# Feed-forward x turned on VectorE in 32x32 blocks by way of DRAM, in place of TensorE transposes

## The chip, the cores and the metric

One core of one Trainium2 chip. The metric is the device time of one execution in microseconds (us). Three executions of the kernel before took 1996.22, 1997.45 and 1999.36 us; the median is 1997.45.

## What is computed

One transformer block on x of 8192 tokens x 512 channels, all float32:

```python
mod = silu(c) @ wmod                       # sa, ca, ga, sb, cb, gb, 512 each
h = layernorm(x) * (1 + ca) + sa
x = x + ga * linear_attention(h)           # causal, 16 heads of 32
h = layernorm(x) * (1 + cb) + sb
gate = h @ w_gate.T / 127                  # hidden size 1536
up = h @ w_up.T / 127
x = x + gb * ((silu(gate) * up) @ w_down.T / 127)
```

The change is about the second layernorm: its result h is wanted with channels on the partitions, while x is loaded with tokens on the partitions.

## The kernel before

The attention works through 16 groups of 512 tokens, the feed-forward behind it through 8 groups G of 1024 tokens (8 tiles of 128). The attention's output goes to the DRAM tensor `x_mid`; the feed-forward reads it from there. Every engine has its program written out by hand, in order, with semaphores between them; groups 1 to 6 of the feed-forward are a loop.

A feed-forward group has 12 **steps** q, one for each block of 128 hidden values, and two **down** phases, one after step 5 and one after step 11. For a step TensorE makes seven products of four matmuls of 512 columns in the order p1(q), p7(q-1), p2(q), p5(q), p4(q-1), p6(q), p3(q) (a Strassen-Winograd scheme: operands are B11, B21, B22 and four sums T1 to T4 of channel and token halves, each for k = 0 and 1). A down phase has 8 down products (one a token tile) of 12 matmuls of 512 columns, in four banks `dn`; p7 and p4 of the last step lie between the first ones, and p1, p2 and p5 of the next half or group lie before the eighth. Bank i % 4 is free for down product i when product i - 4 has been multiplied by the gate row gb (`gate_y`, VectorE).

For a step ScalarE copies partial sums out of PSUM (`save_p1`, `save_p5`, `save_u2`), makes the two silus (`silu1`, `silu2`) and rounds the products to their high parts (`h_high`). VectorE makes `add_c22(q-1)`, `add_c11(q)`, `times_gate2(q-1)`, `times_gate1(q-1)`, then whatever is put aside for this step, and `add_c12(q)`. GpSimd makes the low parts of h (`h_low`) and the residual sums (`residual`), SP issues all DMAs. In the trace add_c11 is L1704, add_c12 L1710, add_c22 L1715, times_gate1 L1721, times_gate2 L1729 and gate_y L1736 on VectorE; silu2 is L1590 and save_u2 L1578 on ScalarE. TensorE's p products are L1868 and its down products L1925.

Operands of the next group are made while this one runs:

- SP loads x of group G + 2 in the second down phase of G (`load_x`, L1405) into eight tiles: four in `xg`, two in `z_exp`, two in `z_relu`.
- VectorE makes statistics in steps 2 to 5 (`norm_stats`, L1681), `norm_var` in step 5, GpSimd the power -1/2 (`rstd_of`, L1492), and VectorE normalises in place, two tiles at a time, behind add_c12(6) and in steps 7, 8 and 9 (`norm_x`, L1697).
- TensorE turns: a **turn** is four transposes of 128x128 into one bank, 512 tokens of 128 channels. There are eight a group (`turn`, L1936): one behind each of the steps 8 to 11, three behind p4(11) and one behind the third down product.
- ScalarE evacuates each turn with scale and bias of the modulation (`evacuate`, L1562): the first three in steps 9, 10 and 11 between h_high and silu2, the fourth behind silu2(11), the others later. Then it rounds the operands to high parts (`high`, L1547).
- VectorE makes the sums T1 to T4 (`sum_of`, L1671) and the low parts (`low`, L1675) behind step 11, mixed with gate_y of the second down phase and, at the end, add_c11 of the next group. T1 for k = 0 waits for three evacuations, the other sums for four.

Group 0 of the feed-forward gets its x in the last two groups of the attention: SP loads each half in one DMA (L404) when its tiles have been stored, VectorE makes its statistics (L757) between other work of the attention, and TensorE turns it (L1097, L1105). Behind this load on SP's queue stand the load of a residual tile (L311), the four stores of a block of k (L319), weights and the load of k (L328).

## Time and profile before

| | |
|---|---|
| runs | 1996.22, 1997.45, 1999.36 us |
| profiled execution | 1998.45 us |
| its span | 1996.7 us |
| granted TensorE clock | 0.998 (mean) |
| TensorE / VectorE / ScalarE / GpSimd busy | 98 / 72 / 45 / 44% |
| DMA | 309.81 MB, mean 155 GB/s |

The span runs from the first to the last instruction of the profiled execution; its time is 1.75 us longer, and 1.0 us above the median of the three. The first feed-forward products lie near 990 us, so about half of the span is attention and half feed-forward. Busy shares are averages over stages with different limits, and a TensorE that is busy need not be at its peak.

### The profile page before, as it was taken

The numbers are of one execution on the slowest core, as the hardware profiler recorded it, in microseconds if no ns is written. First come the engines' busy times: TensorE is split into PE (matmuls) and PEld (weight loads), VectorE is DVE, ScalarE is ACT, GpSimd is POOL, SyncE is SP. The second block draws the span as 40 slices with busy tenths as digits, with TensorE's granted clock in tenths as the row PEclk, the third lists the DMA queues.
The fourth block names the chain that finished last, engine by engine and source line by source line (L and its number), as shares of the span: only waits on it lengthen the run. The fifth ranks groups of instructions, "written<-read, shape, count | busy, mean of one in ns | idle before, by whom it ended". The sixth has DMA issues, their size and how long they took to land. (4 is left out here: it accounts for less than half of the span.)

```text
span 1996.7 us, 43856 instructions
## 1 busy us (share of the span) xinstructions
PE 1960.6 (98%) x16008; PEld 1591.9 (80%) x16008; DVE 1443.1 (72%) x2386; ACT 905.7 (45%) x1542; POOL 877.4 (44%) x718
## 2 busy tenths in 40 slices
PE   7999999999999999999899999999999999999999
PEld 4788888888888888887678888788888888888887
DVE  7977888878788878787865857658576585765744
ACT  5443444344444434443344535445354453544533
POOL 2533544444544444453334443444434444344444
PEclk9999999999999999999999999999999999999999
DMA  7223333444434434432575654656546565465553
GB/s 268 69 91 102 115 123 119 135 130 133 135 100 133 128 125 135 127 110 90 179 263 176 207 187 145 214 170 209 186 144 215 171 210 186 144 214 174 169 168 106
DMA packets 202521, 309.81 MB, mean 155 GB/s; under 512 B 16145, under 2 KB 72977, under 8 KB 202386
## 3 DMA queue, kind: packets, MB, share of 16 engines
q1 hardware_dynamic: 201858, 306.78, 48.1%
q8 instruction: 107, 1.75, 0.4%
q10 hardware_dynamic: 528, 1.05, 0.1%
q14 instruction: 28, 0.23, 0.0%
HBM read 225.19 MB, written 82.58 MB: 154 GB/s over the span
## 5 line engine op out<-in xcount | busy, mean ns | idle before, releaser
L1497 POOL TENSOR_TENSOR h_lo<-y_rows,h_hi 128x512 fp32r<-128x512 f32 x192 | 246.5, 1301 | 367.6 <-ACT h_hi L1595 367.6
L461 POOL TENSOR_TENSOR x_res<-y,x_res 128x512 f32<-128x512 f32 x64 | 86.6, 1353 | 294.0 <-DVE y L872 283.5
L851 DVE TENSOR_TENSOR probs<-sc,causal 128x512 f32<-128x512 f32 x256 | 158.5, 681 | 3.8 <-PE sc L1156 2.6
L612 ACT ACTIVATE z_exp<-pj,qk_neg 128x512 f32<-128x512 f32 x128 | 87.7, 686 | 161.5 <-PE pj L1137 158.0
L1137 PE MATMUL pj<-xt_hi,w_hi 128*128 128x512 f32 x512 | 145.9, 406 | 5.7 <-DVE a_t L861 4.7
L1925 PE MATMUL sc<-wd,h_hi 128*128 128x512 f32 x384 | 150.7, 392 | 0.0
L1925 PE MATMUL sc<-wd,h_lo 128*128 128x512 f32 x384 | 149.6, 389 | 0.0
L450 POOL TENSOR_TENSOR a_lo<-a_t,a_hi 128x512 fp32r<-128x512 f32 x60 | 82.2, 1370 | 144.8 <-ACT a_hi L626 144.8
L1137 PE MATMUL pj<-xt_lo,w_hi 128*128 128x512 f32 x512 | 138.1, 391 | 1.8 <-DVE xt_lo L789 1.8
L1137 PE MATMUL pj<-xt_hi,w_lo 128*128 128x512 f32 x512 | 138.1, 392 | 0.0
L1710 DVE TENSOR_TENSOR r_den<-pj,k_tok 128x512 f32<-128x512 f32 x96 | 66.3, 691 | 97.9 <-ACT k_tok L1578 52.2
L1595 ACT ACTIVATE h_hi<-y_rows 128x512 fp32r<-128x512 f32 x192 | 119.0, 620 | 24.9 <-DVE y_rows L1729 13.4
L1573 ACT ACTIVATE k_tok<-sc 128x512 f32<-128x512 f32 x96 | 56.2, 585 | 158.7 <-PE sc L1868 158.7
L445 POOL TENSOR_TENSOR prod<-k_sum,qt 128x512 f32<-128x512 f32 x64 | 94.1, 1471 | 61.4 <-DVE qt L797 42.5
L597 ACT ACTIVATE xf<-sc,mod_col 128x512 f32<-128x512 f32 x64 | 49.8, 778 | 152.7 <-PE sc L1097 152.7
L1137 PEld LDWEIGHTS pj<-xt_hi,w_hi 128*128 128x128 f32 x512 | 91.8, 189 | 33.1 <-DVE a_t L861 11.0
L1137 PEld LDWEIGHTS pj<-xt_lo,w_hi 128*128 128x128 f32 x512 | 96.2, 188 | 23.3 <-DVE xt_lo L789 2.2
L1568 ACT ACTIVATE kv_diag<-pj 128x512 f32<-128x512 f32 x96 | 57.4, 598 | 123.9 <-PE pj L1868 122.9
L1137 PEld LDWEIGHTS pj<-xt_hi,w_lo 128*128 128x128 f32 x512 | 96.7, 189 | 20.9
L1583 ACT ACTIVATE k_sum<-r_den 128x512 f32<-128x512 f32 x96 | 60.7, 632 | 107.7 <-DVE y_rows L1721 95.0
L1721 DVE TENSOR_TENSOR y_rows<-sc,k_sum 128x512 f32<-128x512 f32 x96 | 66.3, 691 | 55.6 <-PE sc L1868 55.6
L1715 DVE TENSOR_TENSOR bv_row<-sc,kv_diag 128x512 f32<-128x512 f32 x96 | 66.3, 691 | 54.8 <-PE sc L1868 54.8
(248 smaller groups left out, 5390.4 us busy)
## 6 DMA issues: line engine op xcount, KB each, us to landing
w_hi<-parts SPq DMA_DIRECT2D x48, 1024.0 KB, 5.4
w_lo<-parts SPq DMA_DIRECT2D x48, 1024.0 KB, 5.4
x_mid<-x_res SPq DMA_DIRECT2D x96, 256.0 KB, 2.8
x_res<-in_L_attn_x SPq DMA_DIRECT2D x64, 256.0 KB, 2.8
k_dram<-k_block SPq DMA_DIRECT2D x252, 64.0 KB
xg<-in_L_attn_x SPq DMA_DIRECT2D x15, 1024.0 KB, 7.4
x_res<-x_mid SPq DMA_DIRECT2D x60, 256.0 KB, 3.9
full<-x_mid SPq DMA_DIRECT2D x60, 256.0 KB, 3.7
```

The costliest lines, as they stand in the source:

```text
L445: pool.tensor_tensor(out=prod[:, c % 2, :], in0=k_sum[:, c % 2, :], in1=qt[parity][:, c, :], op=ALU.mult).then_inc(prod_ready, 1)
L450: pool.tensor_tensor(out=a_lo[:, :], in0=a_t[:, :], in1=a_hi[:, :].bitcast(F32), op=ALU.subtract).then_inc(a_lo_ready, 1)
L461: pool.tensor_tensor(out=x_res[:, slot, :], in0=y[:, :], in1=x_res[:, slot, :], op=ALU.add).then_inc(y_ready, 1)
L612: act.activation(z_exp[:, n % 2, :], pj[:, n % 2, :], ACT.Relu, bias=qk_neg[:, 1 - kind, c:c + 1], scale=-scale).then_inc(below_ready, 1)
L851: dve.tensor_tensor(out=probs[:, h, :].rearrange("p (c i) -> p c i", c=C), in0=sc[:, h, :].rearrange("p (c i) -> p c i", c=C), in1=causal[ ...
L1137: mm = pe.matmul(to, w[:, k, at:at + P], xt[:, k, :], start=(i == 0), stop=(i == len(passes) - 1))
L1497: pool.tensor_tensor(out=h_lo[b], in0=h[i], in1=h_hi[b].bitcast(F32), op=ALU.subtract).then_inc(h_lo_ready, 1)
L1595: act.activation(h_hi[q % 6 * 2 + i], h[i], ACT.Copy).then_inc(h_hi_ready, 1)
L1710: dve.tensor_tensor(out=c12, in0=sums[1], in1=s12, op=ALU.add).then_inc(c12_ready, 1)
L1715: dve.tensor_tensor(out=c22, in0=xs[q % 2], in1=s5, op=ALU.add).then_inc(c22_ready, 1)
L1721: dve.tensor_tensor(out=h[0], in0=xs[q % 2], in1=gate[0], op=ALU.mult).then_inc(h1_ready, 1)
L1925: mm = pe.matmul(dn[i % 4], as_(part[j * 2 + t // GT][:, rows]), as_(wd[half * 6 + j]), start=(j == 0 and part is h_hi), stop=(j == 5 and ...
```

## The change

x of the next group is no longer transposed by TensorE. SP stores each normalised half (512 tokens) to a new DRAM tensor `xn_dram` and loads it back in 16 blocks a partition, so that one VectorE transpose of 32x32 blocks, 128x2048 in place, puts channels on the partitions. The channels come out regrouped (32 of each quarter on each partition quarter), so the host permutes the rows of the gate and up weights and of the modulation alike, and group 0, which TensorE still turns, is loaded in regrouped order, in pieces of 32 channels (128 bytes). ScalarE's evacuations read SBUF instead of PSUM. `z_exp` and `z_relu` become two halves of one tensor `z`, so that a half of x is one tensor.

```diff
@@ sync, attention: x of feed-forward group 0 @@
-                sp.dma_start(xg[:, :, :], mid_groups[half, :, :, :]).then_inc(x_in, 16)
+                for t in range(GT):
+                    for c in range(C):
+                        sp.dma_start(xg[:, t, c * P:(c + 1) * P].rearrange("p (h e) -> p h e", h=HPC),
+                                     mid_groups[half, :, t, :].rearrange("p (h c e) -> c p h e", h=HPC, c=C)[c]
+                                     ).then_inc(x_in, 16)
@@ sync, feed-forward @@
+        def save_xn(G, second):
+            wait(sp, xn_ready, G * 4 + (2 * second - 2))
+            sp.dma_start(xn_dram[second * GN:(second + 1) * GN, :].rearrange("(t p) d -> p t d", p=P),
+                         xg_halves[second][:, :, :]).then_inc(xn_out[second], 16)
+        def load_blocks(G, second):
+            wait(sp, xn_out[second], G * 16)
+            for h in range(HPC):
+                sp.dma_start(xg_halves[second][h * E:(h + 1) * E, :, :].rearrange("p t (b x) -> p (t b) x", x=P),
+                             xn_dram[second * GN:(second + 1) * GN, h * P:(h + 1) * P].rearrange("(b i) x -> i b x", i=E)
+                             ).then_inc(xb_in[second], 16)
...
                     if not last or q + 4 < HB:
                         load_parts(G, q + 4)
+                    if not last and q in (5, 6):
+                        save_xn(G + 1, q - 5)
+                    if not last and q in (7, 8):
+                        load_blocks(G + 1, q - 7)
@@ scalar @@
-                step(G, q, (lambda i=q - 9: evacuate(G + 1, i, dn[i])) if ahead and q >= 9 else nothing)
+                step(G, q, (lambda: (evacuate(G + 1, 0), evacuate(G + 1, 1))) if ahead and q == 11 else nothing)
...
-            evacuate(G + 1, 3, dn[3])
+            evacuate(G + 1, 2)
+            evacuate(G + 1, 3)
@@ vector @@
+        def turn(G, second):
+            wait(dve, xb_in[second], G * (16 * HPC))
+            blocks = xg_halves[second][:, :, :].rearrange("p t d -> p (t d)")
+            dve.transpose(blocks, blocks).then_inc(xt_ps, 1)
...
-                if ahead and not first and 2 <= q < 6:
-                    norm_stats(G + 1, q - 2)
-                if ahead and q == 5:
+                if ahead and not first and 1 <= q < 5:
+                    norm_stats(G + 1, q - 1)
+                if ahead and q == (5 if first else 4):
                     norm_var(G + 1)
-                if ahead and 7 <= q < 10:
-                    norm_x(G + 1, q - 6)
+                if ahead and q >= 10:
+                    turn(G + 1, q - 10)
...
             times_gate1(G, 5)
+            if ahead:
+                norm_x(G + 1, 0)
+                norm_x(G + 1, 1)
             for i in range(FT - 1):
                 gate_y(G, i)
+                if ahead and i in (3, 4):
+                    norm_x(G + 1, i - 1)
             add_c11(G, 6)
             gate_y(G, FT - 1)
             add_c12(G, 6)
-            if ahead:
-                norm_x(G + 1, 0)
@@ tensor: turn() and its eight calls with their waits are gone @@
```

GpSimd's `rstd_of` moves from behind step 5's low parts to ahead of step 4's (step 5's in group 0).

VectorE at the end of the steps of a looped group, from times_gate2(9) to T1 of the next group. Before:

```order
L1729 TENSOR_TENSOR y_rows<-bv_row,gabo_row 128x512
L1721 TENSOR_TENSOR y_rows<-sc,k_sum 128x512
L1710 TENSOR_TENSOR r_den<-pj,k_tok 128x512
L1715 TENSOR_TENSOR bv_row<-sc,kv_diag 128x512
L1704 TENSOR_TENSOR r_den<-pj,k_tok 128x512
L1729 TENSOR_TENSOR y_rows<-bv_row,gabo_row 128x512
L1721 TENSOR_TENSOR y_rows<-sc,k_sum 128x512
L1710 TENSOR_TENSOR r_den<-pj,k_tok 128x512
L1671 TENSOR_TENSOR full<-xf 128x512
```

Now, from times_gate2(9) on (L1730 is the transpose, L1742 add_c12, L1747 add_c22, L1736 add_c11, L1761 and L1753 the products with the gate, L1697 T1):

```order
L1761 TENSOR_TENSOR y_rows<-bv_row,gabo_row 128x512
L1753 TENSOR_TENSOR y_rows<-sc,k_sum 128x512
L1730 STREAM_TRANSPOSE xg<-xg 128x2048
L1742 TENSOR_TENSOR r_den<-pj,k_tok 128x512
L1747 TENSOR_TENSOR bv_row<-sc,kv_diag 128x512
L1736 TENSOR_TENSOR r_den<-pj,k_tok 128x512
L1761 TENSOR_TENSOR y_rows<-bv_row,gabo_row 128x512
L1753 TENSOR_TENSOR y_rows<-sc,k_sum 128x512
L1730 STREAM_TRANSPOSE z<-z 128x2048
L1742 TENSOR_TENSOR r_den<-pj,k_tok 128x512
L1697 TENSOR_TENSOR full<-xf 128x512
```

A transpose of 2048 columns stands ahead of add_c12 in step 10 and in step 11; what follows step 11 has its old order.

ScalarE in step 11 and behind it, from silu1(11) (L1583) to the fourth evacuation (L1562; L1590 is silu2). Before:

```order
L1583 ACTIVATE k_sum<-r_den 128x512
L1595 ACTIVATE h_hi<-y_rows 128x512
L1578 ACTIVATE k_tok<-sc 128x512
L1595 ACTIVATE h_hi<-y_rows 128x512
L1562 ACTIVATE xf<-sc,mod_col 128x512
L1590 ACTIVATE gabo_row<-r_den 128x512
L1562 ACTIVATE r_den<-state,mod_col 128x512
```

Now, from silu1(11) (L1608) to the fourth evacuation (L1587; L1615 is silu2):

```order
L1608 ACTIVATE k_sum<-r_den 128x512
L1620 ACTIVATE h_hi<-y_rows 128x512
L1603 ACTIVATE k_tok<-sc 128x512
L1620 ACTIVATE h_hi<-y_rows 128x512
L1587 ACTIVATE xf<-xg,mod_col 128x512
L1587 ACTIVATE r_den<-xg,mod_col 128x512
L1615 ACTIVATE gabo_row<-r_den 128x512
L1587 ACTIVATE xf<-z,mod_col 128x512
L1587 ACTIVATE r_den<-z,mod_col 128x512
```

One evacuation stood ahead of silu2(11) and one behind it, two others in earlier steps; now two stand ahead of it and two behind.

SP in the attention's last groups, around the load of x for group 0. Before, and now:

```order
L328 DMA k_tok<-k_dram 128x512
L62 REGISTER_ALU
L62 COMPARE_AND_BRANCH
L404 DMA xg<-x_mid 128x4x512
L311 DMA x_res<-in_L_attn_x 128x512
L319 DMA k_dram<-k_block 32x4x128 x4
L332 DMA x_mid<-x_res 128x512
L328 DMA r_den<-k_dram 128x512
```

```order
L329 DMA k_tok<-k_dram 128x512
L62 REGISTER_ALU
L62 COMPARE_AND_BRANCH
L407 DMA xg<-x_mid 128x4x32 x16
L312 DMA x_res<-in_L_attn_x 128x512
L320 DMA k_dram<-k_block 32x4x128 x4
L333 DMA x_mid<-x_res 128x512
L329 DMA r_den<-k_dram 128x512
```

One DMA has become sixteen; the order behind it is the same.

## Rows read from the trace of the kernel before

**Rows 1.** The page, part 1: busy time, share of the span and instructions.
```profile
PE 1960.6 (98%) x16008; PEld 1591.9 (80%) x16008; DVE 1443.1 (72%) x2386; ACT 905.7 (45%) x1542; POOL 877.4 (44%) x718
```

**Rows 2.** Timeline of TensorE, 1200 to 1206: start us, us, engine, line, operation, out<-in, count.
```profile
1201.09 0.62 PE L1868 MATMUL pj<-xt_hi,w_hi 128*128 128x512 f32 x2
1201.55 0.60 PE L1936 MATMUL num<-ident,xg 128*128 128x128 f32 x4
...
1202.45 0.63 PE L1868 MATMUL sc<-xt_hi,w_lo 128*128 128x512 f32 x2
```

**Rows 3.** Timelines of TensorE and of ScalarE, 1265 to 1269.
```profile
1266.52 0.61 PE L1868 MATMUL sc<-xt_hi,w_hi 128*128 128x512 f32 x2
...
1267.58 0.63 PE L1868 MATMUL sc<-xt_lo,w_lo 128*128 128x512 f32 x2
...
1266.38 0.58 ACT L1578 ACTIVATE k_tok<-sc 128x512 f32<-128x512 f32 x1
```

**Rows 4.** Timeline of TensorE, 1225 to 1275.
```profile
1227.09 0.67 PE L1868 MATMUL sc<-w_hi 128*128 128x512 f32 x2
...
1242.61 0.46 PE L1925 MATMUL sc<-wd,h_hi 128*128 128x512 f32 x1
...
1250.86 0.73 PE L1868 MATMUL sc<-w_lo,w_hi 128*128 128x512 f32 x2
```

**Rows 5.** Timeline of VectorE, 1220 to 1275.
```profile
1220.54 0.69 DVE L1721 TENSOR_TENSOR y_rows<-sc,k_sum 128x512 f32<-128x512 f32 x1 [0.61 <-PE sc L1868]
...
1224.18 1.47 DVE L1671 TENSOR_TENSOR full<-xf 128x512 f32<-128x512 f32 x1 [0.44 <-ACT xf L1562]
...
1226.30 0.68 DVE L1715 TENSOR_TENSOR bv_row<-sc,kv_diag 128x512 f32<-128x512 f32 x1
...
1229.30 1.47 DVE L1671 TENSOR_TENSOR full<-r_den,full 128x512 f32<-128x512 f32 x1
1230.70 1.77 DVE L1675 TENSOR_TENSOR xt_hi<-full,w_lo 128x512 fp32r<-128x512 f32 x1
...
1241.84 0.68 DVE L1736 TENSOR_TENSOR a_t<-sc,ga_row 128x512 f32<-128x512 f32 x1
...
1250.04 0.68 DVE L1704 TENSOR_TENSOR r_den<-pj,k_tok 128x512 f32<-128x512 f32 x1
```

**Rows 6.** The instructions of line 1936: duration ns min/median/max, first and last start us.
```profile
L1936 PE MATMUL num<-ident,xg x28: 270/272/273, 1076.5 to 1825.7; 128*128 128x128 f32 x28
```

**Rows 7.** The tile k_block, same columns.
```profile
L845 DVE STREAM_TRANSPOSE k_block<-kt x63: 662/670/714, 63.4 to 972.8; 128x512 f32<-128x512 f32 x63
```

**Rows 8.** Timeline of ScalarE, 1220 to 1275.
```profile
1223.38 0.77 ACT L1562 ACTIVATE xf<-sc,mod_col 128x512 f32<-128x512 f32 x1
1224.04 0.63 ACT L1590 ACTIVATE gabo_row<-r_den 128x512 f32<-128x512 f32 x1
1224.56 0.77 ACT L1562 ACTIVATE r_den<-state,mod_col 128x512 f32<-128x512 f32 x1
```

**Rows 9.** DMA issues: line, queue, count, size of one, us to landing.
```profile
parts<-r_den SPq DMA_DIRECT2D x48, 256.0 KB, 2.4
```

**Rows 10.** Timeline of SP's DMA issues, 880 to 980.
```profile
895.78 0.39 SPq L404 DMA_DIRECT2D xg<-x_mid  x1
...
946.67 1.77 SPq L319 DMA_DIRECT2D k_dram<-k_block  x4
...
956.47 0.39 SPq L404 DMA_DIRECT2D xg<-x_mid  x1
...
973.58 3.04 SPq L319 DMA_DIRECT2D k_dram<-k_block  x4
```

**Rows 11.** Timeline of VectorE, 880 to 1012.
```profile
908.02 1.86 DVE L757 BATCH_NORM_STATS2 stats<-xg 128x6 f32<-128x512 f32 x3
...
962.17 1.29 DVE L757 BATCH_NORM_STATS2 stats<-xg 128x6 f32<-128x512 f32 x2 [0.45 <-DMA xg<-x_mid]
...
965.28 0.42 DVE L861 TENSOR_TENSOR a_t<-num,r_den 128x256 f32<-128x256 f32 x1 [0.96 <-PE pj L1181]
```

More of the change, by code:

```diff
@@ L1321, in attention, with feed_forward @@
     return Programs(sync, gpsimd, scalar, vector, tensor), signals, shared
-def feed_forward(sem, later, ident, mod_col, half_neg, norm, gb_dram, parts, att, shared, x_mid, out):
+def feed_forward(sem, later, mod_col, half_neg, norm, gb_dram, parts, att, shared, x_mid, xn_dram, out):
     stats, mean_var, var_eps, rstd = norm[1:5]
-    xg, xf, h_hi, h_lo, (blocks, filled), b_hi, b_lo, full, wd, total, saved, gate, h, y, x_res, gb_row, xs, sums, dn = shared
+    xg, xg_halves, xf, h_hi, h_lo, (blocks, filled), b_hi, b_lo, full, wd, total, saved, gate, h, y, x_res, gb_row, xs, sums, dn = shared
     c11, c12, c22 = total
@@ L1636, in body @@
             high(G + 1, T4, 0)
-            for i, bank in ((4, sums[0]), (5, sums[1]), (6, xs[0]), (7, xs[1])):
-                evacuate(G + 1, i, bank)
+            for i in range(4, 8):
+                evacuate(G + 1, i)
             for op in (B11, B21, T1, T2, B22, T3, T4):
@@ L1928, in down @@
                 mm.then_inc(dn_ps, 1)
-        def turn(G, i, bank):
-            k, which = divmod(i, 4)
-            c, second = (k, k + 2, k, k + 2)[which], which // 2
-            wait(pe, xn_ready, G * 4 + (2 * second - 2))
-            for t in range(GT):
-                mm = pe.transpose(bank[:, t * P:(t + 1) * P], xg[second * GT + t][:, c * P:(c + 1) * P], ident[:, :])
-            mm.then_inc(xt_ps, 1)
         def step(G, q):
```

57 lines of the change are left out of this document (23 added, 34 removed).

## The prediction

> **What bounds the kernel now.** I read the page first: TensorE is busy 98% of the span, VectorE 72% [rows 1]. The edit takes 224 transposes off TensorE, so at first sight their time is the gain. The timeline of TensorE gives it. Two matmuls take 0.455 us from start to start. Where four transposes (one turn) lie between p3 of a step and p1 of the next, 1201.09 to 1202.45 is 1.36 us instead of 0.91: a turn costs 0.45 us [rows 2]. But a boundary without a turn is not free either: 1266.52 to 1267.58 is 1.06 us, 0.15 too many, since p7 waits for ScalarE's save_u2, which ends at 1266.96 [rows 3]. So a turn at a step boundary is worth 0.30 us. Of the 8 turns of a group, 3 are followed by a further step and 5 by a down product: 3 x 0.30 + 5 x 0.45 = 3.15 us, in 7 groups 22.0 us. That is the ceiling.
>
> Then I asked what ends TensorE's waits where the last five turns are. Three places touch. p4 of step 11 starts at 1227.09; the c22 that it needs is a VectorE sum that starts at 1226.30 and takes 0.68. The down product of bank 2 starts at 1242.61; the gating that frees its bank starts at 1241.84 and takes 0.68, so it ends 0.09 earlier. p6 of the next group starts at 1250.86; its c11 starts at 1250.04 and ends 0.14 earlier [rows 4, 5]. Between 1224.18 and 1250.7 VectorE has no gap: eight sums, fourteen low parts, six gatings, c22, two products with the gate and c11 run back to back, most of them 0.6 us apart. So in the tail of a group VectorE and TensorE are level, and **VectorE's row of work sets when the next group starts**. Removing TensorE work there gives nothing unless this row also starts or ends earlier. The group's period is 124.9 us: (1825.7 - 1076.5) / 6 [rows 6].
>
> **The change, part by part.**
> *Boundaries of steps 8 to 10.* The turns leave three boundaries, where TensorE is the bound: -0.30 x 3 = -0.9 us per group.
> *The turn on VectorE.* 128x512 costs 0.67 us (63 times, 662 to 714 ns) [rows 7]. Of that some 0.13 is overhead (the next instruction starts 0.6 after it), so 128x2048 is about 4 x 0.535 + 0.13 = 2.3 us. Bounds: 4 x 0.54 = 2.1 below; above, 4 x 1.77 = 7.1, if it were held like the sum with two SBUF inputs at 1230.70, which ran beside a GpSimd instruction [rows 5]. I take 2.3, as it has one input and its own row never shows more than 714 ns. In step 10 it stands after times_gate1 and before add_c12. From the end of p4, which releases times_gate1, TensorE has p6, p3, p1, p7, p2 = 20 matmuls x 0.228 = 4.55 us before p5 wants that sum; 0.69 + 2.3 + 0.69 = 3.7 fit, with 0.9 to spare. Cost 0, up to a turn of about 3.1 us. The Trainium skill speaks against this part: "VectorE: DVE Perf Modes", rules for kernel authors, sends a 128x128 transpose to TensorE where a PSUM destination will do, and its table of transpose paths has 311 ns for 128 bf16 columns on VectorE; by that, as an estimate, a turn would be 16 x 0.311 = 5.0 us. The row of this trace says less than half of it.
> *The evacuations.* This is where the saving goes. Now the third evacuation (1223.38, 0.77 us) comes before silu2 (1224.04), and the first sum, T1, starts at 1224.18, just behind it; the fourth starts at 1224.56 [rows 5, 8]. After the change the first and second stand where the third was and the third and fourth come behind silu2: one evacuation (0.66 from start to start), silu2 (0.52) and again one evacuation (0.66) more before T1, so T1 starts 1.84 us later, at 1226.0. silu2's own sum is ready in time: times_gate1 at 1220.54, turn at 1221.15, add_c12 from 1223.4 to 1224.1. Reading SBUF instead of PSUM I take as equal; bounds 0.52 (the pitch to silu2's successor) and 0.77 each, which is -0.4 to +0.3 us on T1.
> *The row of VectorE behind it.* T1 takes 1.47 us now because GpSimd is in a low part; at 1226.0 GpSimd is done, and it takes 0.68: -0.8. The two long ones that follow (1229.30 and 1230.70) stay, as GpSimd's next low parts move along with their products. The order of the row is the same. So it ends 1.84 - 0.8 = about 1.0 us later, bounds 0.4 and 1.9.
> *Sum per group:* -0.9 + 1.0 = +0.1 us (-0.9 to +1.0), in 7 groups +0.5 us (-6 to +7). TensorE gets to p4, to bank 0 and to bank 2 early and waits there for c22 and the gatings.
> *Normalising and statistics moved.* Four products 0.5 us apart come before gating 0, which waits anyway for its down product more than 5 us; two pairs between gatings 3 and 5 fall in gaps; statistics one step earlier need x by the group's first step, and it is loaded during the down products before; norm_var in step 4 uses about as much as the turn in step 10. Each 0; if they are late, add_c12 is late next.
> *Store and loads through DRAM.* One 1 MB store and four 256 KB loads for each half are issued by SP behind loads of weights; the loads go out two steps, 13 us, before their turn, and 512-byte pieces are no problem: 256 KB in 512 of them lands in 2.4 us [rows 9]. A weight load is issued more than three steps before use. 0.
> *End of the attention.* SP's single load of x for a group of 512 tokens (956.47, landing just after 962) becomes 16 loads of 64 KB in 128-byte pieces [rows 10]. VectorE's statistics are already waiting for it: 0.45 us, start at 962.17 [rows 11]. Four loads of 64 KB take 1.77 us now (0.48 apart), and 3.04 us (0.90) at worst [rows 10]; I take 0.55, as nothing there has so many pieces. The last lands at 956.5 + 15 x 0.55 + 2.4 = 967.1, so VectorE stands 4.9 us longer, of which the gap of 0.96 us at 965.28 [rows 11] and some tenths are taken back: **+3.8 us**. The residual load, the k store and weights queue behind on SP, by 8 us, but their users have moved by nearly 4 and had as much in hand. Bounds: +2.7 at 0.48; at 0.90 the last lands at 972.4, +9.1, and the first such load (895.78, statistics at 908.02) lands at 911.7, +3.7 more: +12.8.
>
> Sum: +0.5 - 0.3 (group 0 runs outside the loop, its boundaries give a little more) + 3.8 = +4.0 us. Against the profiled execution's 1998.45 us that is 2002.5; against the median of the runs, which is 1.0 us below it, 2001.5 us.
>
> **Rivals.**
> *A, the work of TensorE is the bound after all* (faster). Then the full 22.0 us come: 1997.45 - 22.0 + 3.8 = 1979 us. For it: 98% against 72%. Against it: the three touching places. It decides where VectorE's row from T1 to c11 gets 3 us shorter or starts that much earlier.
> *B, VectorE's row starts no later* (evacuations from SBUF quick, or fewer collisions with GpSimd): the boundaries' 0.9 x 7 = 6.3 us come: 1995 us, no change.
> *C, the small pieces bind.* The queue takes 0.90 us a load or more: 1997.45 + 0.2 + 12.8 = 2010.5 us. No row shows 128-byte data. The Trainium skill, "DMA: Bandwidth & Descriptors", specifications, says that below 512 bytes a transfer is not at line rate and is done as a read-modify-write; its figure of 0.95 us for 64 KB would put the sixteenth, as an estimate, at 974.
> *D, the turn is late or slow.* With 7.1 us instead of 2.3 it would overrun step 10 by 4.0 and shift T1 by a further 4.2 us: 7 x 8 = 57 us, 2058; a turn of 4 us would give 7 x 1.9 = 13 us, 2015. Nothing in the rows of the transpose speaks for it; it starts at about 3.0 us.
> *E, the change doesn't do what it says:* excluded for TensorE, the order has no transposes left there.
>
> **How the numbers follow.** Forecast (+0.1 a group, tail +3 to +6) 0.52; A 0.10; B 0.18; C 0.13; D 0.07. A measurement here tells 0.2% (4 us) from no change, so the borders are 1993.45 and 2001.45, and the forecast lies on the upper one. Faster: A, and a third of B with quick evacuations and a short tail, 0.17. Slower: C, D and about half of the forecast's cases, 0.47. Same: 0.36. The range leaves out A and most of D: 1992 to 2011, with B's lower end and C in it.
>
> **What would show it.** Right: 14 transposes of 2.2 to 2.4 us; step periods of 6.54 us throughout; a group's period of 124.3 to 125.6; T1 1.8 us later behind times_gate1 of step 10; TensorE waiting over 1 us for c22 at p4 and for a gating at bank 0; statistics in the last attention group waiting about 5 us for x. Wrong: a period near 121.8 (A), or waits for xn_dram before a transpose, or a transpose over 3 us (D).

## The result and the profile after

The changed kernel takes 2013.28 us (median of four runs, 2011.39 to 2015.96) against 1997.39 us for the kernel before in the same series: a ratio of 1.0079, 95% interval 1.0062 to 1.0097. It is slower by about 16 us, and outside the predicted range. Its profiled execution took 2011.44 us, with a span of 2009.7 us and a mean granted clock of 0.993 [before: 1998.45, 1996.7, 0.998].

The page of the changed kernel, parts 1 and 3, answers to [rows 1]:

```profile
PE 1945.9 (97%) x15784; PEld 1572.1 (78%) x15784; DVE 1476.3 (73%) x2400; ACT 908.8 (45%) x1542; POOL 883.9 (44%) x718
...
q1 hardware_dynamic: 254658, 336.15, 55.3%
```

TensorE lost its 224 transposes, and VectorE has 14 more instructions. They are as long as forecast, though each of the 14 ran beside a GpSimd instruction (groups of VectorE's instructions; last come the mean ns of one and the idle time before them). What was not forecast stands at the end of the first line:

```profile
L1730 DVE STREAM_TRANSPOSE z<-z 128x2048 f32<-128x2048 f32 x7 | 16.2, 2310 | 6.2 <-DMA z<-xn_dram 6.2
L1730 DVE STREAM_TRANSPOSE xg<-xg 128x2048 f32<-128x2048 f32 x7 | 16.1, 2303 | 0.0
```

**Where the time came from.** The starts of add_c11 of each group's first step make a ruler for the feed-forward. They are read off VectorE's timeline (line 1704 before, line 1736 after):

```
                 group 0   then the seven periods to groups 1 ... 7
before            995.59   129.37 125.08 125.13 124.67 124.70 124.64 124.67
after            1004.82   129.63 124.63 127.72 124.53 124.80 124.60 125.06
```

So of the 13.0 us between the two profiled executions 9.2 arose before the feed-forward began and 3.8 in it: 2.6 in the single period 127.72, 1.0 from the last group's first step to the end. The other periods are as before or some tenths shorter. Two places, then.

*The end of the attention.* SP's timeline has the two series of 16 loads, [rows 10] before (start us, us, queue, line, out<-in, count):

```profile
895.74 11.73 SPq L407 DMA_DIRECT2D xg<-x_mid  x16
...
960.96 11.16 SPq L407 DMA_DIRECT2D xg<-x_mid  x16
```

That is 0.73 and 0.70 us per load, not 0.55. VectorE's statistics wait for them (its timeline, [rows 11] before, where the first had no such wait and the second 0.45 us):

```profile
909.33 1.88 DVE L762 BATCH_NORM_STATS2 stats<-xg 128x6 f32<-128x512 f32 x3 [1.28 <-DMA xg<-x_mid]
...
974.06 1.29 DVE L762 BATCH_NORM_STATS2 stats<-xg 128x6 f32<-128x512 f32 x2 [8.34 <-DMA xg<-x_mid]
```

Both series count. At 890 us, ahead of the first, VectorE is where it was in the kernel before, within 0.1 us; at 925 us, behind the first, it is 4.0 us late, and behind the second 9.2. Of the 4.0 only 1.3 is the wait above. The rest comes in two longer waits of VectorE behind it, for TensorE (2.25 us instead of 1.33) and for ScalarE (2.86 instead of 1.08); meanwhile the residual load that stands behind the series on SP's queue goes out at 907.5 instead of 897.2. What holds up the two engines was not followed further.

*The long period.* Group 2's last step on VectorE, answering to [rows 5]:

```profile
1353.92 0.69 DVE L1753 TENSOR_TENSOR y_rows<-sc,k_sum 128x512 f32<-128x512 f32 x1 [0.39 <-PE sc L1903]
1357.98 2.31 DVE L1730 STREAM_TRANSPOSE z<-z 128x2048 f32<-128x2048 f32 x1 [3.37 <-DMA z<-xn_dram]
1360.22 0.65 DVE L1742 TENSOR_TENSOR r_den<-pj,k_tok 128x512 f32<-128x512 f32 x1
1362.27 0.69 DVE L1697 TENSOR_TENSOR full<-xf 128x512 f32<-128x512 f32 x1 [1.40 <-ACT xf L1587]
1363.07 0.69 DVE L1697 TENSOR_TENSOR full<-r_den,full 128x512 f32<-128x512 f32 x1
1363.68 0.68 DVE L1747 TENSOR_TENSOR bv_row<-sc,kv_diag 128x512 f32<-128x512 f32 x1
```

The turn of the second half waits 3.37 us for its blocks. Everything behind it moves: T1 (1362.27), then c22 (1363.68), and TensorE's p4 behind that (its timeline, [rows 4] before):

```profile
1364.41 0.73 PE L1903 MATMUL sc<-w_hi 128*128 128x512 f32 x2 [4.27 <-DVE bv_row L1747]
...
1365.71 0.63 PE L1960 MATMUL sc<-wd,h_hi 128*128 128x512 f32 x1
1366.14 0.63 PE L1960 MATMUL sc<-wd,h_lo 128*128 128x512 f32 x1
```

Behind the stall the matmuls start 0.43 us apart instead of 0.23. The granted clock says why. Windows of that stretch (PE, PEld, DVE, ACT and POOL busy, then granted clock, DMA share, GB/s):

```profile
1356.00:1360.00 4.00, 4.00 (x19) 3.10 (x17) 2.02 (x1) 2.28 (x4) 2.49 (x2) 1.00 1.03 373
1360.00:1364.00 4.00, 0.14 (x1) 0.00 (x0) 2.50 (x5) 2.88 (x5) 0.00 (x0) 1.00 0.16 65
1364.00:1368.00 4.00, 3.59 (x10) 2.82 (x11) 4.00 (x6) 3.74 (x7) 1.43 (x2) 0.64 0.14 19
1368.00:1372.00 4.00, 4.00 (x18) 3.31 (x17) 4.00 (x6) 3.83 (x6) 1.29 (x1) 0.93 0.65 243
```

So 4.27 us of idling were followed by a stretch at the lower of TensorE's two levels, 1.2 GHz. No 2 us window between 1000 and 1880 of the profiled kernel before is under 0.95 of full speed.

SP's timeline tells why the blocks are late. The four loads of the second half took 6.68 us to issue:

```profile
1340.75 0.93 SPq L1399 DMA_DIRECT2D w_hi<-parts  x1
1341.72 6.68 SPq L1423 DMA_DIRECT2D z<-xn_dram  x4
1348.51 3.28 SPq L1399 DMA_DIRECT2D w_lo<-parts  x1
```

The last of them went out near 1348 and the blocks were there at 1357.9. SP's DMA issues have 8.6 and 9.9 us as the median from a load's own issue to its landing:

```profile
xg<-xn_dram SPq DMA_DIRECT2D x28, 256.0 KB, 8.6
z<-xn_dram SPq DMA_DIRECT2D x28, 256.0 KB, 9.9
```

The theory to test: **16 small-piece loads delay the end of the attention; blocks that land late, by amounts that vary, cost the rest, with a stretch at half clock behind each long stall of TensorE; the feed-forward's own balance is as forecast.**

### The profile page after: what moved, and what is told of

Its sections match the earlier page's. It is cut to its first block and busy times, and to the rows that moved or that the text cites. A ratio compares the mean times of both kernels' runs of the same rounds, so it can differ in the third digit from the quotient of the medians.

```text
span 2009.7 us, 43425 instructions
## 1 busy us (share of the span) xinstructions
PE 1945.9 (97%) x15784; PEld 1572.1 (78%) x15784; DVE 1476.3 (73%) x2400; ACT 908.8 (45%) x1542; POOL 883.9 (44%) x718
## 5 line engine op out<-in xcount | busy, mean ns | idle before, releaser
L617 ACT ACTIVATE z<-pj,qk_neg 128x512 f32<-128x512 f32 x128 | 87.8, 686 | 164.0 <-PE pj L1142 153.9
L1742 DVE TENSOR_TENSOR r_den<-pj,k_tok 128x512 f32<-128x512 f32 x96 | 65.7, 685 | 92.4 <-ACT k_tok L1603 68.5
L1608 ACT ACTIVATE k_sum<-r_den 128x512 f32<-128x512 f32 x96 | 60.7, 632 | 106.3 <-DVE y_rows L1753 95.5
L1747 DVE TENSOR_TENSOR bv_row<-sc,kv_diag 128x512 f32<-128x512 f32 x96 | 66.2, 689 | 53.6 <-PE sc L1903 53.5
L1753 DVE TENSOR_TENSOR y_rows<-sc,k_sum 128x512 f32<-128x512 f32 x96 | 66.3, 690 | 49.8 <-PE sc L1903 49.5
```

The costliest lines, as they stand in the source:

```text
L617: act.activation(z_exp[:, n % 2, :], pj[:, n % 2, :], ACT.Relu, bias=qk_neg[:, 1 - kind, c:c + 1], scale=-scale).then_inc(below_ready, 1)
L1747: dve.tensor_tensor(out=c22, in0=xs[q % 2], in1=s5, op=ALU.add).then_inc(c22_ready, 1)
L1753: dve.tensor_tensor(out=h[0], in0=xs[q % 2], in1=gate[0], op=ALU.mult).then_inc(h1_ready, 1)
```

## The experiments

All edits start from the changed kernel unless said otherwise. Ratios are against the kernel before in the same series, with 95% intervals.

### One load per half instead of 16

```
-                for t in range(GT):
-                    for c in range(C):
-                        sp.dma_start(xg[:, t, c * P:(c + 1) * P]..., ...[c]).then_inc(x_in, 16)
+                sp.dma_start(xg[:, :, :], mid_groups[half, :, :, :]).then_inc(x_in, 16)
```

> The changed kernel, with group 0's x fetched by one DMA per half as before instead of 16 with 128-byte pieces; the channels of group 0 are then not regrouped, so its values are not the reference's. Theory (the 16 loads delay the end of attention by the 9.2 us that add_c11(0, 0) moved, 995.59 to 1004.82): add_c11(0, 0) near 995.6 and the time 9 us under the changed kernel's 2011.4, so about 2002, some 4 to 5 us above the kernel before. Rival (the loads only show the shift, which the feed-forward's code or DMAs make): add_c11(0, 0) stays past 1003 and the time is within 2 us of the changed kernel's.

add_c11(0, 0) started at 996.42, so the loads do make the delay. But the time did not follow: 2014.46 us (five runs, 2004.17 to 2017.19), ratio 1.0085 [1.0068, 1.0102]. Only the profiled execution, the fastest, is near the forecast 2002; the others have a granted clock down to 0.990. In it the late blocks sit in groups 0 and 1, not 2: periods 132.75 and 125.89, waits for xn_dram of up to 3.5 us, stretches at the lower clock from 1104 and from 1232. The forecast of the time failed because I had taken the late blocks of one profile as the cost in every run.

### Blocks one step earlier

```
+                    if not last and q in (6, 7):
+                        load_blocks(G + 1, q - 6)
                     if not last or q + 4 < HB:
                         load_parts(G, q + 4)
-                    if not last and q in (5, 6):
-                        save_xn(G + 1, q - 5)
-                    if not last and q in (7, 8):
-                        load_blocks(G + 1, q - 7)
+                    if not last and q == 5:
+                        save_xn(G + 1, 0)
...
                     store(G, i)
+                    if not last and i == 5:
+                        save_xn(G + 1, 1)
```

> The changed kernel, with the blocks of the next group saved and loaded one step earlier, the second half's save before the first's step 6 loads and each pair of block loads ahead of that step's load of parts on SP. Theory (group periods of 124.6 are the floor, the 127.7 of group 2 is a late block): no wait of the transpose for xn_dram of over 0.3 us in any group, no stretch at a granted clock of about 0.6 after steps 10 and 11, every group at 124.5 to 124.8; against the changed kernel's profiled 2011.4 about 3 to 4 us less, 2007.5, and more where its other runs were longer. Rival (the loads stand behind 1 MB of weights anyway, so the parts that now start later are late instead): the blocks land in time, but TensorE waits for parts, and the time stays at 2011 or over. Second rival (the period is set by other transfers in that stretch, and the late blocks are a symptom): group 2 is still at 127 or more.

2005.54 us (2003.73 to 2009.01), ratio 1.0038 [1.0026, 1.0051]. Group 2's blocks are now issued from 1323.6 on for turns at 1344.3 and 1350.9 (SP's timeline):

```profile
1323.56 1.95 SPq L1423 DMA_DIRECT2D xg<-xn_dram  x4
1325.62 0.57 SPq L1399 DMA_DIRECT2D w_lo<-parts  x1
1326.23 5.85 SPq L1423 DMA_DIRECT2D z<-xn_dram  x4
```

No turn waits for xn_dram, no window is under 0.95 of the clock, and from group 1 on all periods lie between 124.47 and 124.73. TensorE did not wait for parts in exchange. Four loads still take 2 us (first half, now ahead of the load of parts) and 5.1 to 6.2 us (second half, behind it) to issue, and 5.5 and 10.4 us (median) to land; they only start sooner. What is left are TensorE's two waits in each boundary, 1000 to 1880, which the kernel before has not (there none of them is over 0.5 us):

```profile
PE sc L1905 <- DVE bv_row L1749: 11.1, 8, 1.5
PE num L1962 <- DVE a_t L1770: 8.7, 7, 1.3
```

### Both

> Both edits together, group 0's values as in the first of these runs. If tail and late blocks are the whole difference, and they add, the time is that of the kernel before within 1.5 us (1997 to 1999), with all periods at 124.5 to 124.8 and no gain from the 56 transposes that left TensorE. If they do not add (the late blocks cost nothing in a run with the shorter tail, or the reverse), it lies with the lower of the two alone. If TensorE's 56 fewer transposes are worth something that the late blocks hid, it is under 1995.

1997.43 us (ten runs, 1995.57 to 2000.09), ratio 0.9993 [0.9983, 1.0002]: the kernel before, though 56 turns of four transposes are off TensorE. So the two causes are the whole of the loss, and there is no gain beneath them. In the profiled execution, the slowest of the ten, the periods from group 2 on are 124.5 to 124.9, but that of group 1 is 126.68: there TensorE waited twice for parts, so here the early blocks did cost something at times (TensorE's waits, 1000 to 1880):

```profile
PE sc L1901 <- DMA w_hi<-parts: 1.2, 1, 1.2
PE sc L1901 <- DMA w_lo<-parts: 0.5, 1, 0.5
```

The two causes are not simply additive in the medians: with blocks early, the 16 loads cost 2005.54 - 1997.43 = 8.1 us; with one load, the late blocks cost 2014.46 - 1997.43 = 17.0 us; both together cost 16 here and 21 in a later series. The late blocks' part varies by more than 10 us between executions, and four or five runs don't pin it.

### 16 loads with pieces of 512 bytes

```
-                        sp.dma_start(xg[:, t, c * P:(c + 1) * P].rearrange("p (h e) -> p h e", h=HPC),
-                                     mid_groups[half, :, t, :].rearrange("p (h c e) -> c p h e", h=HPC, c=C)[c]
+                        sp.dma_start(xg[:, t, c * P:(c + 1) * P],
+                                     mid_groups[half, :, t, c * P:(c + 1) * P]
```

> The changed kernel, whose 16 loads of group 0's x per half take 512-byte pieces instead of four of 128 bytes each; the count of DMAs is the same, the channels are not regrouped, so group 0's values are not the reference's. Theory (each DMA costs SP its issue, whatever its pieces): the 16 issues still take 11 us and the time is within 1.5 us of the changed kernel's. Rival (the 512 small pieces of each DMA fill the queues, and SP waits for room): issues of 0.5 us or less, 16 in under 8 us, and the time 3 to 6 us under the changed kernel's.

The two series of issues now take 8.47 and 8.79 us, 0.53 and 0.55 a load, and add_c11(0, 0) starts at 998.92, 3.3 us later than before instead of 9.2:

```profile
957.46 8.79 SPq L407 DMA_DIRECT2D xg<-x_mid  x16
```
```profile
967.84 1.29 DVE L762 BATCH_NORM_STATS2 stats<-xg 128x6 f32<-128x512 f32 x2 [5.25 <-DMA xg<-x_mid]
```

Neither theory had it whole. Number and piece size both count. The executions differ by up to 1.3 us before the first of these loads, so the delay is better counted from 890 us on: then the 16 loads with long pieces cost 2.4 us, and with 128-byte pieces 9.3 in the change and 7.8 in the version with early blocks. The time, 2011.17 us (2006.49 to 2014.62), ratio 1.0068 [1.0051, 1.0084], says nothing on this, since late blocks are in it: six waits of the turn for xn_dram, 7.5 us in all.

### Fewer transposes on TensorE and nothing else

The kernel before, with one of the four transposes of each turn.

```
-            for t in range(GT):
+            for t in range(1):
                 mm = pe.transpose(bank[:, t * P:(t + 1) * P], ...)
...
-            act.activation(to, bank, ACT.Identity, ...)
+            act.activation(to.rearrange("p (a n) -> p a n", a=GT),
+                           bank[:, 0:P].rearrange("p (a n) -> p a n", a=1).broadcast_to([P, GT, P]), ACT.Identity, ...)
```

> The kernel before, with one of the four transposes of each of its 56 banks left in (168 of 224 gone from TensorE; ScalarE reads the one four times, so the values are not the reference's), and nothing given to VectorE. Theory (the row of sums, lows and gates on VectorE sets each group's period, and TensorE only waits for it longer): group periods of 124.0 to 124.7 and a time 0 to 4 us under the kernel before. Rival (TensorE binds, its whole row counts): 42 transposes of each next group less at about 0.1 us, some 3.4 us by the 0.45 us of a bank with its switch, so periods near 121.5 and the time 20 us under.

1988.13 us (1986.15 to 1988.42), ratio 0.9955 [0.9941, 0.9969]; periods from group 1 on 123.3 to 123.7, in the mean 1.3 us less than before. Both theories missed: 9 us came, where one had 0 to 4 and the other 20, and of three quarters of 3.15 us, 2.4 us, about half comes out. Part of the reason can be read off VectorE's timeline. In the mean of groups 1 to 6, T1 starts 98.2 us after its group's c11 instead of 99.0, 0.7 us sooner, as much as three quarters of the three boundaries' 0.30; and the row from T1 to the next c11 is 0.6 us shorter, 25.2 instead of 25.9, for which no run gives the reason. The other turns, those between down products, became waits: the gating of bank 0 now ends up to 0.8 us too late (waits of TensorE, 1250 to 1880):

```profile
PE num L1926 <- DVE a_t L1737: 3.9, 5, 0.8
```

So TensorE's work ahead of the row's start counts, and its work beside the row is in part taken back by waits for the row.

### The turn cut to almost nothing

The version with both edits, VectorE's transposes cut to one 32x32 column block, waits kept.

```
-            blocks = xg_halves[second][:, :, :].rearrange("p t d -> p (t d)")
+            blocks = xg_halves[second][:, 0, 0:E]
```

> The kernel with one load of group 0's x per half and the blocks loaded early, with VectorE's 14 transposes of 128x2048 cut to 32x32 or 128x32, and all its waits kept; the values are not the reference's. Theory (T1 waits for ScalarE, whose evacuations stand in a fixed place behind h_high, not for the turn): the first of the row's sums starts where it did and periods stay at 124.5, the time within 1 us of the uncut one's 1997.4. Rival (the 2.3 us of the second turn are on the path to the row): periods of 122.3 to 123.5 and the time 7 to 15 us less.

1996.24 us (1994.11 to 1998.48), ratio 0.9997 [0.9987, 1.0006], periods 124.46 to 124.98 (125.79 once): the same as uncut. A turn of 2.3 us costs nothing where it stands, as forecast; T1 waits for ScalarE.

### c22 ahead of the sums

The version with both edits; VectorE idles 2.1 us before T1 while TensorE waits for c22, so c22 goes first.

```
+            add_c22(G, 11)
             sum_of(G + 1, T1, 0)
             sum_of(G + 1, T2, 0)
-            add_c22(G, 11)
```

> The same kernel (one load per half, blocks early), with c22 of step 11 put ahead of T1 and T2 on VectorE, which idles 2.1 us just there. TensorE's wait of 1.5 us for c22 should go. Theory (the row on VectorE ends where it did, and c11 of the next group and the gating at bank 0 stand at its end): the row gets 0.6 us shorter, and the period falls by 0.6 to 1.0, to 123.6 to 123.9, 4 to 7 us in all; the rest of the 1.5 us comes back as a longer wait for the gating of bank 0. Rival (TensorE's waits at the boundary are what sets the period): 1.5 us less per group, periods of 123.0, 10 us in all. Second rival (TensorE has slack there): no change.

A miss: 2001.81 us (2001.38 to 2003.30), ratio 1.0028 [1.0018, 1.0038], 4.4 us *slower* than without this edit, and 5.6 us above the version with the cut turn, which ran in the same series. The wait for c22 is gone, and TensorE reaches bank 0 of the down products that much earlier, while the gating comes as late as before. The two waits of 1.5 and 1.3 us have become one of up to 2.1 us. TensorE's waits, 1000 to 1880:

```profile
PE num L1958 <- DVE a_t L1766: 14.3, 7, 2.1
```

And behind four of these seven waits the clock falls (TensorE's timeline and windows of one of them):

```profile
1611.87 0.50 PE L1958 MATMUL num<-wd,h_hi 128*128 128x512 f32 x1 [2.05 <-DVE a_t L1766]
...
1613.37 0.63 PE L1958 MATMUL num<-wd,h_hi 128*128 128x512 f32 x1
```
```profile
1608.00:1612.00 4.00, 1.95 (x9) 1.26 (x9) 4.00 (x8) 2.62 (x5) 0.02 (x1) 1.00 0.00 0
1612.00:1616.00 4.00, 4.00 (x13) 3.18 (x14) 4.00 (x5) 2.30 (x4) 3.86 (x2) 0.67 0.27 74
1616.00:1620.00 4.00, 4.00 (x18) 3.25 (x17) 4.00 (x6) 0.00 (x0) 1.67 (x1) 0.90 0.67 223
```

Summed over the 2 us windows, what is missing to full clock is 6.8 us for the four. The ruler shows where it goes. The periods that follow a boundary with such a stretch are 125.37, 126.45 and 125.81; those that follow a boundary without one are 124.70, 124.06 and 124.99, in the mean 124.6. So a stretch costs the next period about 1.3 us, and where the clock stayed full the edit brought nothing: 124.6 lies within the 124.5 to 124.9 of the version without it.

### The gating sooner

To see whether the lower clock hangs on that wait, the gating of bank 0 was moved three places up in the row.

```
-            for op in (T2, B22, T3, B11, B21, T4):
+            for op in (T2, B22, T3, B11):
+                low(G + 1, op, 0)
+            gate_y(G, FT)
+            for op in (B21, T4):
                 low(G + 1, op, 0)
             sum_of(G + 1, T1, 1)
-            gate_y(G, FT)
```

> The version with c22 first (one load per half, blocks early), and the gating of dn bank 0 three places sooner in VectorE's row, ahead of the low parts of B21 and T4 and of the sum T1(1); the row holds the same operations. Theory (the version with c22 first lost its gain because its two waits met in one of 2.0 to 2.1 us, after which four of seven boundaries ran at TensorE's lower clock): the wait for the gating is 0.2 to 0.6 us, no stretch runs at the lower clock, and the gain that was forecast comes out, periods of 123.3 to 123.9 and a time of 1989 to 1993. Rival (the lower clock there has another cause, the end of the row or transfers): stretches at the lower clock remain and the time is over 1998. Second rival (the row's end at c11 of the next group sets the period, whatever TensorE waits for before): no lower clock, but periods of 124.1 to 124.5 and 1994 to 1998.

A miss too: 2005.83 us (2004.83 to 2007.28), ratio 1.0044 [1.0027, 1.0060]. The wait at bank 0 shrank to 0.2 us as meant, but the gating of bank 1, which I had left where it was, took its place, with nearly as long a wait, 1.8 us six times and 1.9 once, and again four of seven boundaries fell to the lower clock:

```profile
PE sc L1960 <- DVE y L1766: 12.8, 7, 1.9
...
PE num L1960 <- DVE a_t L1766: 1.7, 7, 0.2
```
```profile
1236.00:1240.00 4.00, 2.19 (x10) 1.48 (x10) 3.96 (x7) 2.57 (x5) 0.84 (x2) 1.00 0.43 131
1240.00:1244.00 4.00, 4.00 (x12) 3.19 (x11) 4.00 (x4) 0.36 (x1) 2.50 (x2) 0.57 0.41 131
```

The run doesn't decide between its theories as they were put, because its edit didn't remove the stall. Nor is it clear why it is 4 us slower than the run before it, whose waits and stretches at the lower clock sum to as much: between the two profiled executions it is 2.6 us, half of it there before the feed-forward. Again the periods behind a boundary with a stretch are the long ones, 126.14, 126.11 and 126.11 against 124.83, 125.26 and 124.81. It does show that the drop goes with the stall wherever this is (bank 0 at 1611.87, bank 1 at 1239.15, p4 at 1364.41), and that rearranging inside a row whose start and end stay put only moves the waits.

### The row earlier

The changed kernel with blocks early; turns in steps 9 and 10, an evacuation each in steps 9 and 10 and two in step 11, T1 inside step 11, so that c22 stands behind one sum instead of two, the low part of B22 ahead of times_gate1(11), and the gating of bank 0 ahead of the sum T1 for k = 1.

```
@@ scalar @@
-            for q in range(7, HB):
-                step(G, q, (lambda: (evacuate(G + 1, 0), evacuate(G + 1, 1))) if ahead and q == 11 else nothing)
+            for q in range(7, HB - 1):
+                step(G, q, (lambda: evacuate(G + 1, q - 9)) if ahead and q >= 9 else nothing)
+            save_p1(G, 11)
+            if ahead:
+                evacuate(G + 1, 2)
+            save_p5(G, 11)
+            if ahead:
+                evacuate(G + 1, 3)
+            silu1(G, 11)
...
-            evacuate(G + 1, 2)
-            evacuate(G + 1, 3)
@@ vector @@
-                if ahead and q >= 10:
-                    turn(G + 1, q - 10)
+                if ahead and q in (9, 10):
+                    turn(G + 1, q - 9)
+                if ahead and q == 11:
+                    sum_of(G + 1, T1, 0)
...
-            sum_of(G + 1, T1, 0)
             sum_of(G + 1, T2, 0)
             add_c22(G, 11)
...
             low(G + 1, T1, 0)
+            low(G + 1, B22, 0)
             times_gate1(G, 11)
             sum_of(G + 1, T4, 0)
-            for op in (T2, B22, T3, B11, B21, T4):
+            for op in (T2, T3, B11, B21, T4):
                 low(G + 1, op, 0)
+            gate_y(G, FT)
             sum_of(G + 1, T1, 1)
-            gate_y(G, FT)
```

> The changed kernel with the 16 loads of group 0's x as they are, blocks early, and the boundary written anew: turns in steps 9 and 10, one evacuation each in steps 9 and 10 and two in step 11, T1 inside step 11, c22 ahead of the other sums, the gating of bank 0 one place earlier. Theory (the period is set by when VectorE's row begins and how long it is): the row begins some 2 to 2.5 us earlier and both of TensorE's waits of 1.3 and 1.5 us go, periods of 121.8 to 122.3; 2.4 us by 7 groups off the 2005.5 of the version with early blocks alone, so 1987 to 1990 (the 6.9 us of the attention's end are still in it). Rival (the blocks land too late for a turn in step 9): waits for xn_dram come back and periods stay over 124. Second rival (POOL's h_low or the residuals bind once the row is short): periods of 123 to 124.

1988.98 us (1987.75 to 1991.10), ratio 0.9965 [0.9952, 0.9977], with periods of 122.15 to 122.37 from group 1 on: 2.3 us less than 124.5, as forecast, though the slow end of the attention is still in it (add_c11(0, 0) at 1003.94). Of TensorE's waits at the boundary one of 0.4 us is left, and no window is under 0.95 of the clock.

### The row earlier, and group 0 regrouped in DRAM

Besides, four DMAs per half copy x_mid to xn_dram in regrouped order, one per tile in groups 1 and 14 of the attention, and the load at the end is a single one.

```
+        def regroup(half, c):
+            ...
+            sp.dma_start(xn_dram[half * GN:(half + 1) * GN, c * P:(c + 1) * P].rearrange("n (h e) -> n h e", h=HPC),
+                         x_mid[half * GN:(half + 1) * GN, :].rearrange("n (h c e) -> c n h e", h=HPC, c=C)[c]
+                         ).then_inc(regrouped[half], 16)
...
-                for t in range(GT):
-                    for c in range(C):
...
+                sp.wait_ge(regrouped[half], 16 * C)
+                sp.dma_start(xg[:, :, :], xn_groups[half, :, :, :]).then_inc(x_in, 16)
```

> The version with the boundary written anew (row early, blocks early) and, besides, group 0's x regrouped in DRAM: four DMAs per half from x_mid to xn_dram, one per tile in groups 1 and 14 of attention, 128-byte pieces, and one contiguous load per half at the end; the output is the reference's. Theory (the 16 issues in a row on SP cost the end of attention 6.4 to 9.2 us, the copies lie beside attention's work): add_c11(0, 0) near 995.6, periods of 122.2, and a time of 1981 to 1983, 0.75% under the kernel before. Rival (2048 pieces per copy hold SP's queue so long that attention's k_dram round trips of that tile come late): attention loses 1 to 3 us in each of groups 1 and 14, and 1984 to 1988.

**1983.02 us** (1981.53 to 1984.90), ratio **0.9924 [0.9911, 0.9938]**: 15 us under the kernel before and 30 under the change (36 under the change's runs of the same series, below), with nothing of the computation left out. add_c11(0, 0) is at 997.33, 1.7 us later than forecast: the second load now waits until the last copy has landed, and VectorE's statistics wait 5.35 us for it. A copy of 2048 pieces holds SP for 0.54 to 0.59 us, and the load is back to one (SP's timeline; [rows 10] before):

```profile
956.63 0.54 SPq L344 DMA_DIRECT2D xn_dram<-x_mid  x1
960.76 0.38 SPq L417 DMA_DIRECT2D xg<-xn_dram  x1
```

The row at group 2's end (VectorE's timeline; [rows 5] before). T1 stands before c22 and even before c12 of step 11:

```profile
1341.88 0.69 DVE L1718 TENSOR_TENSOR full<-xf 128x512 f32<-128x512 f32 x1 [0.22 <-PE sc L1926]
1343.47 0.69 DVE L1763 TENSOR_TENSOR r_den<-pj,k_tok 128x512 f32<-128x512 f32 x1 [0.90 <-ACT k_tok L1615]
1344.08 0.74 DVE L1718 TENSOR_TENSOR full<-r_den,full 128x512 f32<-128x512 f32 x1
1345.41 0.69 DVE L1768 TENSOR_TENSOR bv_row<-sc,kv_diag 128x512 f32<-128x512 f32 x1 [0.59 <-PE sc L1926]
...
1368.85 0.68 DVE L1757 TENSOR_TENSOR r_den<-pj,k_tok 128x512 f32<-128x512 f32 x1
```

T1 starts 95.5 us after its group's c11 (1246.35), where it was 99.2 before and 100.1 after the change (group 1 of each); T2, behind which the row runs nearly without a gap, starts after 97.7 instead of 100.7 and 100.9. TensorE waits once in that boundary, for 0.40 us. Its busy share of the span is 98% again, now with its transposes gone.

> The changed kernel with blocks early and group 0's x regrouped in DRAM as in the run beside it; the boundary as the change has it. Theory (late loads and late blocks are the whole of the 16 us): as the version with one load and early blocks, 1997.4, so within 0.2% of the kernel before, add_c11(0, 0) near 995.6 and periods of 124.5. Rival: the copies cost attention more than the 6.4 us they save, and it stays over 2003.

The same copies with the boundary as the change has it: 1999.61 us (1999.04 to 2001.03), ratio 1.0009 [1.0000, 1.0018], add_c11(0, 0) at 997.74 and periods of 124.5 to 124.9. Mending both causes gives back the kernel before, no more; the 16.6 us between this and the version above are the boundary written anew, its earlier start and its new order together.

### The change once more

> The changed kernel itself, unchanged, for a second profile and more runs. Theory (a late block costs 3 us and more whenever the loads behind the parts come late, which varies from execution to execution, and TensorE's clock falls to its lower level after each stall of over 2 us): other groups are late than group 2, each with a wait of the transpose for xn_dram of over 1.5 us, a stall of TensorE of over 2 us and a stretch at half clock behind it; the granted clock of all its runs lies under 0.995. Rival (something fixed in group 2): the same group is late, and the spread of its runs is that of the kernel before.

2018.96 us (2013.11 to 2023.73), ratio 1.0099 [1.0080, 1.0119]. This time the long periods are those of group 0 (135.01), group 5 (126.63) and group 2 (125.91), with stretches at the lower clock from 1116 and from 1748; the mean clock is 0.991. In group 0 the turn of the second half waited 5.02 us, and TensorE behind it 6.05:

```profile
1113.47 2.31 DVE L1730 STREAM_TRANSPOSE z<-z 128x2048 f32<-128x2048 f32 x1 [5.02 <-DMA z<-xn_dram]
```
```profile
1120.00 1.22 PE L1903 MATMUL sc<-w_hi 128*128 128x512 f32 x2 [6.05 <-DVE bv_row L1747]
```

In group 2 the turn waited 1.49 us and TensorE 2.40, and there the clock stayed full, against the expectation:

```profile
1371.09 0.73 PE L1903 MATMUL sc<-w_hi 128*128 128x512 f32 x2 [2.40 <-DVE bv_row L1747]
```

The end of the attention was later as well, 1008.19, 12.6 us behind the kernel before. Which group is late varies; that some are doesn't. All waits of turns for xn_dram in this execution sum to 11.2 us (9.8 and 1.4), and its time beyond the late start of the feed-forward is 2019.0 - 1996.7 - 12.6 = 9.7 us; in the first profile they sum to 6.2 us, against 3.8. So a late block costs about what the turn waits for it, less the tenths that the other periods gained. The expectation had more for it, the stretch at half clock besides; but behind a late block VectorE's row is late by the same wait, and TensorE has those microseconds to spare.

## Why the prediction was wrong

The forecast was 2001.5 us (1992 to 2011), the result 2013.3. By its steps:

*The feed-forward's balance: right.* Boundaries, turn, evacuations and VectorE's row summed to +0.1 us a group. The version without the two disturbances has periods of 124.5 to 124.9 from group 2 on, against 124.6 to 125.1 before, and the ratio 0.9993. In detail (group 1 of the change): the turn takes 2.31 us (forecast 2.3), T1 starts 100.1 us after its group's c11 instead of 99.2 (forecast +0.9), takes 0.69 instead of 1.47, and the row from T1 to c11 is 24.5 us long instead of 25.9. TensorE waits 1.5 us for c22 and 1.2 for the gating of bank 0, both over 1 us as forecast. That the row sets the period was shown from both sides: with the transposes gone from TensorE and the row no sooner the period stayed, and with the row's boundary written anew, TensorE's work the same, it fell by 2.3 us. TensorE's work ahead of the row counts too: a quarter of the transposes left in gave half their time.

*End of the attention, "+3.8 us": the mechanism right, the term mis-sized.* "I take 0.55" per load is exact for pieces of 512 bytes: measured 0.53 and 0.55, a wait of the statistics of 5.25 us (forecast 0.45 + 4.9) and +3.3 at add_c11(0, 0). The 128-byte pieces make it 0.70 to 0.76 and the wait 8.34; and the first series, which I priced only at the upper bound, gives 4.0 of the +9.2 (between 6.4 and 12.6 in other profiles). That is inside the bounds of +2.7 to +12.8 but far from the value taken. The row that it was nearest to, the DMAs of k_dram (stores, which the prediction calls loads), has as few and as long pieces as the 512-byte version. The direction was that of rival C. The Trainium skill, "DMA: Bandwidth & Descriptors", specifications, says that transfers below 512 bytes are not at line rate. The runs agree as far as the 16 issues take 11.2 to 12.2 us with 128-byte pieces and 8.5 to 8.8 with 512-byte ones.

*Store and loads through DRAM, "0": the step that failed.* The argument was that the loads go out 13 us ahead and that 256 KB in 512-byte pieces land in 2.4 us. The 2.4 us of [rows 9] are of stores, not loads, and of the attention (220 to 887 us); the same page has 3.7 and 3.9 us for loads of 256 KB from x_mid in the feed-forward. Behind 1 MB loads of parts the four loads took 2.5 to 3.9 us to issue for the first half and 5.1 to 6.7 for the second, and each landed 8.6 and 9.9 us (median) after its own issue: from the first issue of the second half to its last landing 13.0 to 16.2 us, as long as the lead or longer. I had put "waits for xn_dram before a transpose" under the signs of being wrong, and gave late turns 0.07; they are what happened. This term is worth 3.8 and 9.7 us in the two profiles of the change, 7.7 and 17.0 between medians (16 loads and one), and varies between executions. It is also what puts the time outside the range: with the blocks in time and the 16 loads left the median is 2005.5, inside it; with one load and the blocks late it is 2014.5.

*Missing altogether:* what a stall does to TensorE's clock. Behind late blocks it cost little, as VectorE's row was later still. In the version with c22 first it cost the next period about 1.3 us each time, some 5 us for four, which is about what that version lost; its periods behind boundaries at full clock, 124.6 in the mean, show no gain that it could have hidden.

*Rival A* was put as deciding "where VectorE's row gets 3 us shorter or starts that much earlier". With the row 3.7 us earlier than before the periods are 122.1 to 122.5, near the 121.8 of that case. It is true of this design, but not of this order of its work. Not run was the kernel before with its row that much earlier and the transposes still on TensorE; so how much of the 15 us needs them gone is open.

## What to carry to other kernels

When work leaves the busiest engine and nothing gets faster, look for the row on another engine that begins late: here the work was gone and nothing came of it until the row's first operation moved up by 4.6 us, and its unbroken part by some 3. A transfer's lead must be set against its issue time and landing in the stretch where it runs, behind what is queued ahead of it, and not against the same size elsewhere; one profile of a kernel with a thin lead shows only which groups were late that time. Joining two short waits of TensorE into one long one can cost more than it saves, as with c22 first.

## What was not expected of the hardware

- At a stall TensorE's granted clock can fall to its lower level, in the feed-forward for 3.4 us, or 6.8 at the waits of 6.05 us and, with one load, 4.42 us, where it fell some 2 us before the wait was over. It did so at every wait of 2.3 us and more in the profiles of the change and of the versions with one load and with 512-byte pieces except one: a wait of 2.40 us at 1112.07 of the first profile of the change had it, one of 2.40 us at 1371.09 of the second did not. It did so at four of seven waits of 2.0 to 2.1 us, and at four of seven of 1.8 to 1.9 us, where the longest of the seven was not among the four; so the length of the wait alone doesn't decide it. Where each of seven boundaries had two waits of 1.5 and 1.3 us, 8.5 us apart, it did not once (early blocks, both edits, and the copies in DRAM). One such stretch behind a wait of 2 us lacks about 1.7 us to full clock (6.8 us over four).
- A DMA of 64 KB costs SP's queue 0.53 to 0.55 us an issue with 128 pieces of 512 bytes and 0.70 to 0.76 with 512 pieces of 128 bytes, 16 in a row; but a copy within DRAM of 256 KB in 2048 such pieces costs 0.54 to 0.59. What makes the difference between the two was not tried.
- Four loads of 256 KB in 512-byte pieces take 2 us to issue ahead of a load of 1 MB, and 2.5 to 7.5 us behind one (7.5 with one load and with both edits).
